# Gated cross-attention block on one core: VectorE's and ScalarE's orders around new weights, straight-line steps, and squares summed by ScalarE

## The reference

```python
ln_out = _ln(hidden_states, ln_w, ln_b)
q  = _ln(_fp8_linear_pertensor(ln_out, wq,  ...), qln_w, qln_b)      # layer norm over each head
k  = _ln(_fp8_linear_pertensor(ln_out, wk,  ...), kln_w, kln_b)
v  =     _fp8_linear_pertensor(ln_out, wv,  ...)
core = _gqa(q, k, v)
qx = _ln(_fp8_linear_pertensor(ln_out, wqx, ...), qxln_w, qxln_b)
kx, vx = jnp.split(jnp.einsum('bsi,oi->bso', cond, w_kv_x), 2, axis=-1)
kx = _ln(kx, kxln_w, kxln_b)
xout = _gqa(qx, kx, vx)
catq = _div_clamp_fp8(jnp.concatenate([core, xout], axis=-1), proj_smooth)
return jnp.einsum('bsi,oi->bso', catq, wproj) * (proj_in_scale * proj_w_scale)
# around it: x + tanh(g) * attention, then x + tanh(g) * a mixture of 8 experts, 2 per token
```

## Time and profile before

| | |
|---|---|
| median of 3 runs | 1248.5 us (1246.94 to 1249.56) |
| profiled execution | 1250.32 us, of it the span 1248.6 us |
| PE busy | 1105.4 us, 89% of the span |
| DVE busy | 841.9 us, 67% |
| ACT busy | 705.0 us, 56% |
| POOL busy | 487.5 us, 39% |

### The profile page before, as it was taken

How to read it: one execution, slowest core, us unless ns; L and a number is a source line. 1 busy time by engine, 2 the same in 40 slices (tenths; PEclk the granted TensorE clock), 3 DMA queues, 4 the chain that set the end, 5 groups by cost and what they waited for, 6 DMA issues and landing times. The chain is left out here.

```text
span 1248.6 us, 21647 instructions
## 1 busy us (share of the span) xinstructions
PE 1105.4 (89%) x5656; PEld 903.2 (72%) x5656; DVE 841.9 (67%) x1704; ACT 705.0 (56%) x1794; POOL 487.5 (39%) x584
## 2 busy tenths in 40 slices
PE   1089999899999989999988999996899839999996
PEld 1068888677888767888867888874788727777875
DVE  7968787786888687877778787767344665655100
ACT  7966878645888746678764665662122503343432
POOL 3075445343454534445434443331000313655442
PEclk9589999999999999999999999999899859999998
DMA  5041111114111113211111411110546155766220
GB/s 195 6 185 44 41 34 57 38 37 170 46 44 42 33 48 135 85 33 49 50 33 33 141 42 40 34 40 9 196 141 243 64 196 179 237 180 180 47 43 1
DMA packets 51737, 107.61 MB, mean 86 GB/s; under 512 B 5985, under 2 KB 26465, under 8 KB 49569
## 3 DMA queue, kind: packets, MB, share of 16 engines
q1 hardware_dynamic: 46912, 97.00, 23.7%
q0 software_dynamic: 4704, 9.18, 3.3%
HBM read 91.48 MB, written 16.52 MB: 86 GB/s over the span
## 5 line engine op out<-in xcount | busy, mean ns | idle before, releaser
L810 PE MATMUL p_proj<-w_hi,xqs 128*128 128x512 f32 (+2 forms) x464 | 158.5, 361 | 54.9 <-DVE w_lo L533 46.4
L608 POOL TENSOR_TENSOR c_lo<-c_raw,c_hi 128x500 fp32r<-128x500 f32 x96 | 143.3, 1493 | 158.0 <-ACT c_hi L659 157.8
L837 PE MATMUL p_proj<-w_hi,c_hi 128*125 128x512 f32 x384 | 165.9, 432 | 7.9 <-POOL c_lo L608 7.9
L602 POOL TENSOR_TENSOR rs<-va,mhalf 125x2 f32<-125x2 f32 (+1 forms) x180 | 154.6, 859 | 15.6 <-POOL va L595 2.9
L595 POOL TENSOR_TENSOR va<-ss,epst 125x2 f32<-125x2 f32 (+1 forms) x180 | 59.9, 333 | 251.8 <-DVE ss L1006 251.7
L837 PE MATMUL p_proj<-w_hi,c_lo 128*125 128x512 f32 x384 | 151.5, 395 | 0.0
L837 PE MATMUL p_proj<-w_lo,c_hi 128*125 128x512 f32 x384 | 151.4, 394 | 0.0
L810 PE MATMUL p_proj<-w_lo,xqs 128*128 128x512 f32 (+2 forms) x464 | 148.8, 339 | 0.0
L810 PEld LDWEIGHTS p_proj<-w_hi,xqs 128*128 128x128 f32 (+1 forms) x464 | 86.7, 187 | 70.3 <-issue 52.6
L1006 DVE TENSOR_REDUCE ss<-sq 125x2 f32<-125x256 f32 (+1 forms) x180 | 89.3, 497 | 46.3 <-ACT sq L669 43.4
L730 ACT ACTIVATE pcross<-p_cross,nmax 112x375 f32<-112x375 f32 x128 | 73.2, 579 | 53.7 <-DVE nmax L1035 50.6
(11 more groups left out here) (237 smaller groups left out, 2755.5 us busy)
## 6 DMA issues: line engine op xcount, KB each, us to landing
c_raw<-in_ctxT SPq DMA_DIRECT2D x96, 250.0 KB, 2.6
shared<-in_w_in SPq DMA_DIRECT2D x16, 1024.0 KB, 9.6
shared<-in_wproj SPq DMA_DIRECT2D x32, 256.0 KB, 2.8
raw_g<-in_Wg SPq DMA_DIRECT2D x8, 1024.0 KB, 6.6
raw_u<-in_Wu SPq DMA_DIRECT2D x8, 1024.0 KB, 7.6
raw_d<-in_Wd SPq DMA_DIRECT2D x8, 1024.0 KB, 5.6
cat_scratch<-cat SPq DMA_DIRECT2D x32, 224.0 KB, 2.0
shared<-cat_scratch SPq DMA_DIRECT2D x2, 1792.0 KB, 8.5
```

The source lines that it names most:

```text
L602: pool.tensor_tensor(rs[0:rows, lo:hi], va[0:rows, lo:hi], mhalf[0:rows, lo:hi], ALU.pow).then_inc(rs_done, 1)
L608: pool.tensor_tensor(flat(c_lo[:, k, :, :]), flat(c_raw[:, k, :, :]), flat(c_hi[:, k, :, :]).bitcast(F32), ALU.subtract).then_inc(cl_done, 1)
L810: m = pe.matmul(out, xqs[:, n, k, 0:rows], (w_hi, w_lo)[i % 2][:, k, lo:lo + w], start=(i == 0), stop=(i == 2 * KB - 1))
L837: m = pe.matmul(bank[0:CT, :], a[:, ch, k, :], w[:, k, CKX:CV], start=(i == 0), stop=(i == 3 * KB - 1))
```

## The change

- **No loop.** `passes` runs `for gp in range(GP - 1)` in Python: PE, DVE, ACT and POOL get every step written out. SP keeps its loops.
- **Sums on ScalarE.** For j = 3 to 5 the one `Square` of 256 columns and VectorE's reduction are replaced by two `Square` of 128 columns, each with `accum_out` into its own column of `ss`. GpSimd's `rstd` then waits for ScalarE instead of VectorE. j = 0 to 2 stay.
- **Ordinary steps, ScalarE.** `take(s, 0)` comes ahead of `turned(t, 1)`, and `turned(t, 2)` ahead of `c_high(s, 0)`.
- **Around new weights.** In "queries" ScalarE takes `c_high` of step 7's first block ahead of `take(s, 5)`, GpSimd its `c_low` ahead of `rstd(s, 5)`, VectorE `w_low` 0 ahead of `scale(s, 5)`. In step 7 GpSimd makes both `c_low` before any `rstd`; VectorE makes `w_low` 1 in two halves, one first, one later with `w_low` 2 between the two `smoothed`, then `w_low` 3, and rounds only in the next step. In "new" ScalarE's `w_high` 4 comes first, and VectorE rounds the earlier step in two pieces: `exponents` (three instructions) ahead of `max_self`, `rounded` (two) behind `norm_cross(t, 1)`.

```diff
+def rd_no(pos, j):
+    return 3 * TJ * pos[0] + 3 * pos[1] + j + 1
...
+    sqx = sb(c, "sqx", [P, NC, 2 * HD], BF16)
...
-        with eng.Fori(0, GP - 1) as gp:
+        for gp in range(GP - 1):
...
         def rstd(s, j):
-            pool.wait_ge(rd_done, st_no(s, j))
+            if j < 3:
+                pool.wait_ge(rd_done, rd_no(s, j))
+            else:
+                pool.wait_ge(pj_done, pj_no(s, j))
...
+                rstd(s, 3)
+                rstd(s, 4)
+                if s[1] == TJ - 1:
+                    c_low((s[0], B - 1), 0)
+                rstd(s, 5)
+            else:
+                c_low(s, 1)
+                c_low(s, 2)
                 for j in range(3, 6):
                     rstd(s, j)
-                if s[1] == TJ - 1:
-                    c_low((s[0], B - 1), 0)
-            else:
-                c_low(s, 1)
-                rstd(s, 3)
-                c_low(s, 2)
-                rstd(s, 4)
-                rstd(s, 5)
...
+        def summed_squares(s, j):
+            act.wait_ge(va_done, st_no(before(s), j))
+            col = STAT[j][1]
+            for h in range(2):
+                last = act.activation(sqx[0:CT, j - 3, h * HD:(h + 1) * HD], p_proj[0:CT, j % 2, h * HD:(h + 1) * HD], ACT.Square,
+                                      scale=float(HD) ** -0.5, accum_out=ss[0:CT, col + h:col + h + 1])
+            last.then_inc(pj_done, 1)
...
+            if change == "new": w_high(g, 4, change)
             if Qt: turned(t, 0)
+            if A: take(s, 0)
             if Qt: turned(t, 1)
-            if change == "new": w_high(g, 4, change)
-            if A: take(s, 0)
+            if Qt: turned(t, 2)
             if A: c_high(s, 0)
-            if Qt: turned(t, 2)
...
+            if A and s[1] == TJ - 1: c_high((s[0], B - 1), 0)
             if A: take(s, 5)
-            if A and s[1] == TJ - 1: c_high((s[0], B - 1), 0)
...
+        def w_low_half(g, n, half):
+            v.wait_ge(wh_done[n], g + 1)
+            (lo, hi), ks = USED[n], slice(2 * half, 2 * half + 2)
+            last = v.tensor_tensor(w_lo[:, ks, lo:hi], w_raw[:, ks, lo:hi], w_hi[:, ks, lo:hi].bitcast(F32),
+                                   ALU.subtract)
+            if half == 1:
+                last.then_inc(wl_done[n], 1)
```

More of the change, by code:

```diff
@@ L510, in attention @@
     dv = sem(c, "dve_chain1")
+    rnd = sem(c, "rnd_chain")
     block = c.enter_context(nc.Block())
@@ L659, in c_high, with squares @@
             act.activation(flat(c_hi[:, k, :, :]), flat(c_raw[:, k, :, :]), ACT.Copy).then_inc(ch_done, 1)
[L661 to L669, removed]
-                           scale=float(HD) ** -0.5).then_inc(pj_done, 1)
+        def squares(s, j, n):
+            if j == 2:
+                act.wait_ge(rd_done, rd_no(s, 0))
+            elif s is not FIRST:
+                act.wait_ge(rd_done, rd_no(tile_before(s), 2 - j))
+            act.activation(sq[:, j % 2, 0:n], p_proj[:, j % 2, 0:n], ACT.Square,
+                           scale=float(HD) ** -0.5).then_inc(pj_done, 1)
+        def summed_squares(s, j):
[5 more added lines that the diff above has]
+            last.then_inc(pj_done, 1)
         def take(s, j):
@@ L681, in take @@
                 act.activation((nq, nqx)[j][:, :], bank, ACT.Copy)
-                squares(s, j, P, 512)
+                squares(s, j, 512)
             elif j == 2:
@@ L687, in take @@
                     act.activation(nk[:, :], bank[:, 0:256], ACT.Copy)
-                    squares(s, j, P, 256)
+                    squares(s, j, 256)
                 else:
@@ L693, in take @@
                 act.activation(valx[0:CT, par, j - 3, :], bank[0:CT, 256:512], ACT.Copy)
-                squares(s, j, CT, 256)
+                summed_squares(s, j)
         def turned(t, n):
@@ L970, in _ @@
     def _(v):
-        v.sem_inc(rd_done, ST0)
         v.sem_inc(ln_done, ST0)
@@ L978, in _ @@
         v.sem_inc(ya_done, 2)
-        CH = 9
+        CH = 5
         def smooth_of(g):
@@ L1001, in sums @@
             v.wait_ge(pj_done, pj_no(s, j))
-            if j >= 3:
-                v.wait_ge(va_done, st_no(before(s), j))
-            elif s is not FIRST:
+            if s is not FIRST:
                 v.wait_ge(va_done, st_no(tile_before(s), j))
@@ L1078, in last_step @@
         def last_step(s, t, g, change):
-            if change == "keys": w_low(g, 1)
+            if change == "keys": w_low_half(g, 1, 0)
             max_self(t)
@@ L1086, in last_step @@
             norm_cross(t, 1)
-            sums(s, 3)
             take_self(t)
@@ L1093, in last_step @@
             max_cross(t, 3)
-            sums(s, 4)
             norm_cross(t, 2)
@@ L1101, in last_step @@
             smoothed(t, 0)
-            sums(s, 5)
+            if change == "keys": w_low_half(g, 1, 1)
+            if change == "keys": w_low(g, 2)
             smoothed(t, 1)
             scale(s, 5)
-            if change == "keys": w_low(g, 2)
-            rounded(t)
+            if change == "keys":
+                w_low(g, 3)
+            else:
+                exponents(t)
+                rounded(t)
         def step(s, t, g, change, k):
@@ L1112, in step @@
                 return last_step(s, t, g, change)
-            if change == "new": w_low(g, 3)
             if A: sums(s, 0)
@@ L1116, in step @@
             if A: sums(s, 1)
+            if change == "new": exponents(before(t))
             if Q: max_self(t)
@@ L1123, in step @@
             if Q: norm_cross(t, 1)
+            if change == "new": rounded(before(t))
             if Q: take_self(t)
@@ L1134, in step @@
             if A: inputs((s[0], s[1] + 1))
-            if A: sums(s, 3)
             if Q: smoothed(t, 0)
@@ L1139, in step @@
             if A: scale(s, 3)
-            if A: sums(s, 4)
             if Q: smoothed(t, 1)
             if A: scale(s, 4)
-            if A: sums(s, 5)
             if change is None and g is not None and s[1] <= KB: weights.means(v, g, s[1] - 1)
+            if change == "queries": w_low(g, 0)
             if A: scale(s, 5)
-            if change == "queries": w_low(g, 0)
+            if Q: exponents(t)
             if Q: rounded(t)
@@ L1154, in step @@
                 for j in range(6):
-                    sums(s, j)
+                    if j < 3:
+                        sums(s, j)
                     if j > 0:
```

22 lines of the change are left out of this document (12 added, 10 removed).

## The result

The changed kernel takes 1238.6 us (median of 4 runs, 1237.8 to 1241.2) against 1249.0 (4 runs, 1246.9 to 1249.6): ratio 0.992, 95% interval 0.990 to 0.994. It is faster, by 10 us and not by the 39 of the forecast, and outside the range of 1200 to 1230. The profiled execution took 1238.48 us, span 1236.6.

A forecast was written before the change was run, and what follows sets the result against it. TensorE, busy nine tenths of attention, was taken as the bound, so only its own waits counted. Gains of 7.4 + 6.7 + 18.4 + 7.8 less 1.3 made 39.0 us: from 1250.3 to 1211.3, as median 1209, range 1200 to 1230.

The forecast's parts named there:

- I take 0.35 a step: Ordinary steps, squares of q ahead of qxT: the sq wait of 0.40 goes; 7.4 us gained, ends 0 and 8.4.
- R3: Ordinary step: c_lo holds VectorE's scaling of q, pself late by 0.47 a step, 0.40 not won; 1228 us, chance 0.11.
- I leave 0.3 of wait each: Step "new": rounding ahead of max_self and behind norm_cross leaves 0.3 us of wait each; 7.8 of 8.7 gained.
- The half clock: Stretches before the new weights: half clock followed TensorE's idle time and goes with it, counted within the 18.4 us gained.
- R1: Boundaries at new weights: waits come back, each keeps 3.5 us more, 10.5 in all; 1220 us, chance 0.20.
- R4: Context blocks: ScalarE becomes the bound through the pairs of squares; slower, 1281 to 1300 us, chance 0.04.
- Value 0: Sums on ScalarE: a pair takes 0.66 us, both engines are off the path, so no time gained or lost.
- c_high and c_low earlier: Step 7's first context block: the 1.67 us wait for c_lo goes in four passes; 6.7 us gained.
- VectorE's order in step 7: Before the new weights: pself wait shrinks from 2.46 to between 0 and 0.8, w_lo's 1.83 goes; 18.4 us gained.
- No loop: Loop's end: TensorE's waits of 1.70 and 1.1 us in two rounds go, 2.8 us gained within the 8.7.
- the price of 1.3 for straight code: Ordinary stretches written out take 24.24 us against 24.16; 16 more such lose 1.3 us.
- All else: Rest of the span outside the listed attention stretches: forecast change of -0.4 us.

The follow-up runs named there:

- the last experiment: Against the changed kernel with c_hi, scaling, rounding and next-input copies moved (1207.5 us): two rounding instructions of "queries" left for step 7; 1210.8 us, ratio 0.970.

## Why the prediction failed, point by point

- **"I take 0.35 a step" (squares of q).** This step failed first. The gain at the scores was read rightly, the wait is gone. But the step counted 0.37 us of margin left at `pself` and said that the later `c_lo` "may use that up in some steps". It does so in all of them: 0.98 (1.66 - 0.68) against 0.37. R3 gave the stretch rightly (24.6), by a sum that was partly wrong: the 0.40 at the scores is won, and about as much is lost at `kxT`, which R3 didn't have. It got a chance of 0.11, because "TensorE doesn't show it". The trace before has 1.21 in 8 of 28 scalings, and TensorE does show them: the ordinary stretches with one take 24.24 to 24.32, most others 24.17. It has 1.47 in one ordinary step, and there the stretch took 24.55, with a wait of 0.17 for `kxT`. Most of the 0.53 (1.21 - 0.68) fitted into the margin that the change took away. And with nothing held the term is worth 0.27, not 0.40 (24.16 to 23.89), since `kxT` is late even so.
- **Step "new": "I leave 0.3 of wait each".** It failed by 14 us over three boundaries. That three instructions stand ahead of `max_self` was seen, and priced by their own 1.2; with a `c_lo` beside them they take 2.1. The two ahead of `pselfT` were taken as covered, and are not. The half clock, which was to go with the old stalls, came back with the new ones; each time it adds 1.5 us or more.
- **Rivals as alternatives.** R3 and R1's mechanism (exponents ahead of `max_self`) came together. The sum of their prices, 18.7 + 10.5 on top of 1209.5, is 1238.7 and lay outside a range made from each alone. That it meets the measured time is in part luck, since R3's sum left out what is won at the scores and lost at `kxT`. (R4's 1281 to 1300 starts from the profiled execution, not the median, and is 1.8 too high; nothing hangs on it.)
- **"Value 0" for the sums on ScalarE** had the wrong size: alone they are worth 7.3 us, most of it through GpSimd, which then waits one engine less. In the changed kernel this overlaps with the earlier `c_high` and `c_low`: both are there to remove the same wait for c_lo. Those two without the sums were not run. ScalarE's cost was overrated: a `Square` with its accumulator follows the other after 0.25, a pair takes 0.50 and not 0.66, and ScalarE's busy time grew by 21 us (705.0 to 726.4), not 30 or more:

```profile
129.28 0.26 ACT L685 ACTIVATE sqx<-p_proj 125x128 bf16<-125x128 f32 x1
129.44 0.20 ACT L685 ACTIVATION_READ_ACCUMULATOR sqx<-p_proj 125x1 f32 x1
129.53 0.27 ACT L685 ACTIVATE sqx<-p_proj 125x128 bf16<-125x128 f32 x1
```

- **c_high and c_low earlier:** the mechanism was right, no wait is left. The 6.7 show as 4.0, since the same stretches carry the loss at `pself` and `kxT`. With the scaling moved it is gone, and they take 22.11 each, 6.75 less than before in all.
- **VectorE's order in step 7:** right, 15.5 of 18.4; the wait for w_lo is gone, that for `pself` 0.73, clock 1.00. How much of the 15.5 is this order's alone is open, as the sums on ScalarE alone gave 4.8 in these stretches. What stays of that wait is not VectorE's order, as the last experiment shows; that it is ScalarE's is read from its trace and was not tried.
- **No loop:** 2.8 was forecast for the waits, and 3.0 measured alone; the price of 1.3 for straight code was no price of the code.
- **All else**, taken as unchanged, is 5.8 us shorter. Over the eleven other traces these stretches spread from 497.4 to 504.0, with the half-clock stretches of the projection and the end lying differently in each. Why they differ was not settled.

## What to carry to other kernels

When an edit gives an engine's consumer less slack, list every collision that the trace shows harmless today, and price it against the slack that is left, in each step and not "in some". Where two engines exclude each other, look at what the one that loses has queued behind the contested instruction: here moving that instruction behind two others was worth more than moving the other engine's work. Rivals at different places add up, and a range has to hold their sum.

## What the runs showed of the hardware that was not expected

- The scaling, a VectorE instruction with two operands in SBUF, and GpSimd's `c_lo` exclude each other for the whole of one. Which goes first flips on little. In the loop `c_lo` starts 0.5 us ahead of the scaling and yet takes 2.31 while the scaling takes 0.68; in the same steps written out it takes 1.24 and the scaling 1.21. The loop as such does not decide it: with ScalarE's sums only, the loop is there, and `c_lo` goes first in every step. The Trainium skill (SBUF — State Buffer, section Who interferes with whom) says that issue order decides who blocks; the rows of the straight code agree, those of the loop don't, by the starts that the profile shows. The two in the loop:

```profile
165.40 2.31 POOL L608 TENSOR_TENSOR c_lo<-c_raw,c_hi 128x500 fp32r<-128x500 f32 x1 [0.16 <-ACT c_hi L659]
```

```profile
165.90 0.68 DVE L1015 TENSOR_TENSOR nq<-nq,rs 128x512 f32<-128x512 f32 x1
```

- The loop's back edge (the jump from its end to its start) cost TensorE 1.5 us in each of two rounds. By the Trainium skill (Advanced Engine Details and Errata, section Control Flow Timing) a compare-and-branch is some 108 ns; the loop's end took far more here. What it spends the rest on, no run shows.
- After stalls of 1.5 and 0.3 us close together, in most rounds with a third of 0.6 to 0.8 behind them, the granted clock fell to 1.2 GHz for 3.4 to 6.8 us in 11 of 12 rounds of four kernels; with 0.5 and 0.7 us, 11 us apart, it stayed at 2.4.
